# D groups first on TensorE, x_b tiles behind the gathers, and q weights made by VectorE for chunks 0 to 3

## The reference, cut to what matters

```
base = inputs                                   # (512, 40, 16): batch b, feature i, embedding d
curr = base
for Wk, bk in ((W0, b0), (W1, b1), (W2, b2)):
    z    = einsum('bid,bjd->bdij', base, curr)
    curr = einsum('bdij,ijh->bhd', z, Wk) + bk[None, :, None]
    logit.append(curr)
pooled = sum(concatenate(logit, axis=1), axis=-1)
out = pooled @ lin_w + lin_b                    # (512, 1)
```

## Time and profile before

| | us |
|---|---|
| median of 3 runs (185.47 to 185.96) | 185.86 |
| the profiled execution, its own time | 186.29 |
| its span from first to last instruction | 184.5 |
| TensorE busy (matmuls, 814) | 175.8 (95%) |
| VectorE busy | 151.8 (82%) |
| ScalarE busy | 73.9 (40%) |
| GpSimd busy | 16.2 (9%) |
| the 16 DMA engines, mean over the span | 204 GB/s |

### The profile page before, as it was taken

How to read it: one execution, slowest core, us unless ns; L and a number is a source line. 1 busy time by engine, 2 the same in 40 slices (tenths; PEclk the granted TensorE clock), 3 DMA queues, 4 the chain that set the end, 5 groups by cost and what they waited for, 6 DMA issues and landing times.

```text
span 184.5 us, 2573 instructions
## 1 busy us (share of the span) xinstructions
PE 175.8 (95%) x814; PEld 118.7 (64%) x814; DVE 151.8 (82%) x135; ACT 73.9 (40%) x79; POOL 16.2 (9%) x21
## 2 busy tenths in 40 slices
PE   7798998869999999999999999999999999999994
PEld 2364474546677777777777777777777777777760
DVE  0699698869999999999999999999999999300622
ACT  2554664124444624462446244534453445002001
POOL 3670010087000000000000000000000000000000
PEclk9999999999999999999999999999999999999999
DMA  6999997999797739774986597659765200000000
GB/s 192 379 409 411 412 219 218 231 406 397 230 324 233 234 122 321 247 227 124 331 230 228 126 322 235 223 135 329 228 219 128 99 0 0 0 0 4 0 0 0
DMA packets 11845, 37.71 MB, mean 204 GB/s; under 512 B 2305, under 2 KB 2941, under 8 KB 11838
## 3 DMA queue, kind: packets, MB, share of 16 engines
q1 hardware_dynamic: 11538, 37.38, 62.1%
q0 software_dynamic: 48, 0.16, 0.3%
q10 hardware_dynamic: 252, 0.09, 0.3%
HBM read 36.28 MB, written 1.33 MB: 204 GB/s over the span
## 4 chain that ended last, share of the span: by engine, by line
PE 79%; DMA 8%; SPq 3%; POOL 3%; issue 2%; DVE 1%; ACT 1%; DVEq 0%; ACTq 0%
PE q_ps L434 39%; PE c_ps L434 36%; DMA pair_sb<-d_dram 3%; DMA pair_sb<-w_pairs 3%; DMA d_dram<-w_d 2%; PE q_ps L518 2%; SPq L153 2%; POOL pair_sb L401 1%; POOL wq_low L424 1%; PE q_ps L443 1%; POOL wc_low L406 1%; DVE xb_z L246 1%; ACT z_high L324 1%; SPq L159 1%; PE c_ps L565 1%
## 5 line engine op out<-in xcount | busy, mean ns | idle before, releaser
L324 ACT ACTIVATE z_high<-xb_z 126x1024 fp32r<-126x1024 f32 x56 | 59.2, 1060 | 73.0 <-DVE xb_z L246 69.3
L253 DVE TENSOR_TENSOR z_low<-xb_z,z_high 126x1024 fp32r<-126x1024 f32 x56 | 68.9, 1232 | 1.1 <-ACT z_high L324 0.8
L246 DVE TENSOR_TENSOR xb_z<-x_a,xb_z 126x1024 f32<-126x1024 f32 x50 | 62.1, 1242 | 8.3 <-DMA xb_z<-xw 8.3
L434 PE MATMUL q_ps<-z_high,wq_high 126*101 126x512 f32 x108 | 34.1, 396 | 3.0 <-POOL wq_low L424 1.5
L434 PE MATMUL c_ps<-z_high,wc_high 126*101 126x512 f32 x112 | 35.5, 398 | 0.2 <-issue 0.2
L434 PE MATMUL c_ps<-z_high,wc_low 126*101 126x512 f32 x112 | 35.0, 394 | 0.0
L434 PE MATMUL c_ps<-z_low,wc_high 126*101 126x512 f32 x112 | 35.0, 394 | 0.0
L434 PE MATMUL q_ps<-z_high,wq_low 126*101 126x512 f32 x108 | 33.8, 394 | 0.0
L434 PE MATMUL q_ps<-z_low,wq_high 126*101 126x512 f32 x108 | 33.7, 393 | 0.0
L434 PEld LDWEIGHTS q_ps<-z_high,wq_high 126*101 126x101 f32 x108 | 17.7, 165 | 10.8 <-POOL wq_low L424 2.0
L434 PEld LDWEIGHTS c_ps<-z_high,wc_high 126*101 126x101 f32 x112 | 18.0, 165 | 9.0 <-issue 1.6
(11 more groups left out here) (56 smaller groups left out, 66.1 us busy)
## 6 DMA issues: line engine op xcount, KB each, us to landing
xb_z<-xw SPq DMA_DIRECT2D x50, 512.0 KB, 4.5
x_a<-xa SPq DMA_DIRECT2D x8, 512.0 KB, 5.0
w_d<-w2h SPq DMA_DIRECT2D x4, 512.0 KB, 7.4
w_post<-w1x SPq DMA_DIRECT2D x3, 512.0 KB, 10.0
d_dram<-w_d SPq DMA_DIRECT2D x4, 252.5 KB, 4.3
w_post<-w1x SPq DMA_DIRECT2D x1, 562.5 KB, 12.7
pair_sb<-d_dram SPq DMA_DIRECT2D x6, 82.9 KB
pair_sb<-w_pairs SPq DMA_DIRECT2D x1, 404.0 KB, 5.4
```

Source lines behind the costliest of these rows:

```text
L246: nc.vector.tensor_tensor(xb_z[0:K, c, :], x_a[0:K, u % 2, :], x_b, ALU.mult).then_inc(z_done, 1)
L253: nc.vector.tensor_tensor(z_low[0:K, m % SLOTS, :], xb_z[0:K, c, :], z_high[0:K, m % SLOTS, :].bitcast(fp32), ALU.subtract).then_inc(low_d ...
L324: nc.scalar.activation(z_high[0:K, m % SLOTS, :], xb_z[0:K, m % C, :], ACT.Copy).then_inc(high_done, 1)
L434: last = nc.tensor.matmul(ps[0:J, h * B:(h + 1) * B], w[0:K, c * J:(c + 1) * J], z[0:K, slot, h * B:(h + 1) * B], start=(c == 0 and k == 0 ...
```

## The change

It does three things. On TensorE all five D groups stand ahead of `c1_chunk(0, 1)`, with `select_xb(6)` between the second and the third. On the SP queue `load_xb(1, 2)` moves from behind the D stores to between the gathers of piece 0 and piece 1, and `load_xb(1, 3)` from there to behind piece 1. `first_weights` is now run twice on VectorE, for chunks 0, 1 at m = 10 and for chunks 2, 3 at m = 12, and now behind `split(m-1)`; GpSimd keeps chunks 4 to 6 and has semaphores of its own for them.

```diff
-PREP_AT = 9
+PREP_AT = (10, 12)
...
             store_d(sp, 0, LEFT + 4 * GI, 4 * GI, LOWER - 4 * GI, d_stored)
-            sp.wait_ge(low_done, 3)
-            load_xb(1, 2)
             sp.wait_ge(equals_cleared, 1)
...
             for side, t, piece in GATHER:
                 if piece == 1 and (side, t) == (0, 0):
-                    sp.wait_ge(low_done, 4)
-                    load_xb(1, 3)
+                    sp.wait_ge(low_done, 3)
+                    load_xb(1, 2)
                 if side == 0 or piece > 0:
                     gather_d(sp, side, t, piece)
-            for c in range(4, C):
+            for c in range(3, C):
                 sp.wait_ge(low_done, c + 1)
                 load_xb(1, c)
...
-            def first_weights():
+            def first_weights(i):
-                cols = slice(PREP_CUTS[0] * J, PREP_CUTS[1] * J)
-                dve.wait_ge(dpair_loaded[0], 16 * sum(g[2] == 0 for g in GATHER))
+                cols = slice(PREP_CUTS[i] * J, PREP_CUTS[i + 1] * J)
+                dve.wait_ge(dpair_loaded[i], 16 * sum(g[2] == i for g in GATHER))
...
-                    if m == PREP_AT:
-                        first_weights()
                     if m > 1:
                         split(it, m - 1)
+                    if m in PREP_AT:
+                        first_weights(PREP_AT.index(m))
...
-            for i in range(1, len(PREP_CUTS) - 1):
-                cols = slice(PREP_CUTS[i] * J, PREP_CUTS[i + 1] * J)
-                if PREP_CUTS[i] in WQ_CUTS:
-                    piece = WQ_CUTS.index(PREP_CUTS[i])
-                    pool.wait_ge(dpair_loaded[piece], 16 * sum(g[2] == piece for g in GATHER))
-                    pool.wait_ge(wq_ready, 1)
...
+            cols = slice(PREP_CUTS[2] * J, PREP_CUTS[3] * J)
+            pool.wait_ge(dpair_loaded[1], 16 * sum(g[2] == 1 for g in GATHER))
...
-                if m in PREP_CUTS[:-1]:
+                if m in PREP_CUTS[:2]:
                     pe.wait_ge(wq_ready, PREP_CUTS.index(m) + 1)
+                if m == PREP_CUTS[2]:
+                    pe.wait_ge(last_ready, 1)
...
             d_group(0)
             d_group(1)
-            c1_chunk(0, 1)
+            select_xb(6)
             d_group(2)
             d_group(3)
-            select_xb(6)
             d_group(4)
-            for m in range(2, LAG):
+            for m in range(1, LAG):
                 c1_chunk(0, m)
```

More of the change, by code:

```diff
@@ L133, in build @@
         wq_sums, wq_highs, wq_ready = sem("wq_sums"), sem("wq_highs"), sem("wq_ready")
+        last_sums, last_highs, last_ready = sem("last_sums"), sem("last_highs"), sem("last_ready")
         filled, equals_cleared = sem("filled"), sem("equals_cleared")
@@ L273, in split_x @@
                                         ALU.subtract).then_inc(xa_split, 1)
-            def first_weights():
-                cols = slice(PREP_CUTS[0] * J, PREP_CUTS[1] * J)
-                dve.wait_ge(dpair_loaded[0], 16 * sum(g[2] == 0 for g in GATHER))
+            def first_weights(i):
+                cols = slice(PREP_CUTS[i] * J, PREP_CUTS[i + 1] * J)
+                dve.wait_ge(dpair_loaded[i], 16 * sum(g[2] == i for g in GATHER))
                 nc.vector.tensor_tensor(q_sides[0:K, 0, cols], q_sides[0:K, 0, cols], q_sides[0:K, 1, cols],
                                         ALU.add).then_inc(wq_sums, 1)
-                dve.wait_ge(wq_sums, 1)
+                dve.wait_ge(wq_sums, i + 1)
                 nc.vector.tensor_copy(wq_high[0:K, cols], q_sides[0:K, 0, cols]).then_inc(wq_highs, 1)
-                dve.wait_ge(wq_highs, 1)
+                dve.wait_ge(wq_highs, i + 1)
                 nc.vector.tensor_tensor(wq_low[0:K, cols], q_sides[0:K, 0, cols], wq_high[0:K, cols].bitcast(fp32),
@@ L412, in _ @@
             store_d(pool, 1, 0, UPPER - LEFT, LEFT, d_stored_pool, (0, 32))
-            for i in range(1, len(PREP_CUTS) - 1):
-                cols = slice(PREP_CUTS[i] * J, PREP_CUTS[i + 1] * J)
-                if PREP_CUTS[i] in WQ_CUTS:
-                    piece = WQ_CUTS.index(PREP_CUTS[i])
-                    pool.wait_ge(dpair_loaded[piece], 16 * sum(g[2] == piece for g in GATHER))
-                    pool.wait_ge(wq_ready, 1)
[L419 to L425, removed]
+            cols = slice(PREP_CUTS[2] * J, PREP_CUTS[3] * J)
+            pool.wait_ge(dpair_loaded[1], 16 * sum(g[2] == 1 for g in GATHER))
+            nc.gpsimd.tensor_tensor(q_sides[0:K, 0, cols], q_sides[0:K, 0, cols], q_sides[0:K, 1, cols],
+                                    ALU.add).then_inc(last_sums, 1)
+            pool.wait_ge(last_sums, 1)
+            nc.gpsimd.tensor_copy(wq_high[0:K, cols], q_sides[0:K, 0, cols]).then_inc(last_highs, 1)
+            pool.wait_ge(last_highs, 1)
+            nc.gpsimd.tensor_tensor(wq_low[0:K, cols], q_sides[0:K, 0, cols], wq_high[0:K, cols].bitcast(fp32),
+                                    ALU.subtract).then_inc(last_ready, 1)
         @block.tensor
```

## The result

| | before | changed |
|---|---|---|
| median, us (4 runs each) | 185.73 | 194.68 |
| lowest to highest | 185.47 to 185.96 | 194.22 to 195.01 |
| profiled execution | 186.29 | 194.22 |
| its span | 184.5 | 192.4 |

The ratio is 1.048, with a 95% interval of 1.0449 to 1.0512: slower, as forecast, and 0.4 us from the forecast of 194.3. The two profiled executions are 7.9 us apart and the medians 8.95; the changed kernel's was the fastest of its four.

A forecast was written before the change was run, and what follows sets the result against it. The start of q_chunk(2) on TensorE was taken to set the end: 8.8 us later, less 0.3 of short gaps, net 8.5, gives a median of 194.3 us. The range takes in 191.8 and 196.9.

The forecast's parts named there:

- D groups first: TensorE's D groups ahead of c1_chunk(1): fourth copy 0.87 us earlier, gathers 0.9 us earlier, from 27.2 instead of 28.11.
- form(9): On VectorE: its x_b tile, in the slot of the old load_xb(1, 3), lands at 33.8 us; VectorE idles some 5 us.
- form(10): On VectorE: its tile, in the slot of the old load_xb(1, 4), lands at 37.7 us; start at 37.8.
- GpSimd beside VectorE: GpSimd's weights of chunks 4 to 6 stretch VectorE's work beside them: 0.5 us, bounds nothing and 1.3.
- The first weights: On VectorE behind form(10) and split(9): q_chunk(0) starts at 41.3 us, 41.8 with GpSimd's term, instead of 33.10.
- The clock: TensorE idles over 10 us before q_chunk(0) and falls to 1.2 GHz; return costs 1.7 us, bounds 0 and 3.4.
- The sum: TensorE's q_chunk(2) at 41.8 + 5.7 + 1.7 = 49.2 against 40.44, 8.8 us later; net 8.5 us.
- The rival in which the tiles don't gate: load_xb(1, 3) lands by 31 us, so q_chunk(0) starts at 34.5; 185.4 us, 2%.
- the one in which the clock stays up: Same wait, but TensorE restarts at full speed, q_chunk(2) at 47.6, 7.2 us later; 192.8 us, 10%.

The follow-up runs named there:

- the run that removes it: The changed kernel with 44 more warm-up matmuls on TensorE between c1_chunk(7) and q_chunk(0); ratio 1.0388, 192.86 us.

## Why the prediction was right, by its own steps

*D groups first* was the term that failed in its mechanism. The fourth copy came at 21.46, 0.3 us earlier than before and not 0.87, because D group 3 (the row at 20.34) waited for its piece of w1, which I had not looked at:

```profile
21.46 0.73 ACT L337 ACTIVATE w_d<-q_ps 128x505 f32<-128x505 f32 x2 [0.77 <-PE q_ps L518]
```

The third copy, ahead of that wait, did come 0.82 us earlier. Seven other traces with this TensorE order show the same wait; in the trace of the D groups alone there is none. The gathers came 0.5 us earlier, where I had taken 0.9. Even the 0.5 is not clear of what two executions differ by: with the D groups at their old place the first gather is at 27.42 in the run with the SP order alone and at 28.11 in the trace of before. (And the DMA engines' slackest microsecond beside the stores is the one from 27 to 28, at 75% and not 82%.)

*form(9)* was forecast at 33.8 and started at 33.23; *form(10)* at 37.8 and started at 37.65. The slots were right, and the old landing times a fair measure, but that it came out so closely is in part luck. The gathers came 0.4 us later than I had taken, and the tiles made up for it by landing 4.3 and 5.3 us after their issue, where the old ones took 5.3 and 6.1. In the four other traces with this SP order form(9) starts between 32.85 and 34.18 and form(10) between 37.01 and 38.41.

*GpSimd beside VectorE* was put at 0.5 us and was 0.74, 0.11 on form(10) and 0.62 on split(9). VectorE ran beside GpSimd's subtraction and not its add, which stood alone:

```profile
36.59 0.81 POOL L414 TENSOR_TENSOR pair_sb<-pair_sb 126x303 f32<-126x303 f32 x1 [13.29 <-DMA pair_sb<-d_dram]
...
37.98 1.68 POOL L419 TENSOR_TENSOR wq_low<-pair_sb,wq_high 126x303 fp32r<-126x303 f32 x1
```

The size of 0.5 was luck, because I read rows 9 wrongly. The Trainium skill, SBUF — State Buffer, section Who interferes with whom, would have the loser blocked for a whole instruction. I took that to mean the full 1.8 us of GpSimd's add and so set it aside. But the recorded 1.8 us can hold GpSimd's own wait. The same subtraction takes 0.84 us where it begins just ahead of VectorE's form (the row at 38.37 above) and 1.68 here, where it begins 0.92 us before form(10) gives way to split(9). It ends at 39.66, 0.76 us behind the start of split(9), which takes 0.62 longer. In the rows of before the add ends at 40.35 + 1.82 = 42.17, 0.78 us behind the start of the form at 41.39, which takes 0.65 longer. So the rows agree with that section: VectorE loses what is left of GpSimd's instruction once its own turn comes, in these rows at most some 0.8 us, and not 1.8.

*The first weights* follow: q_chunk(0) forecast at 41.8, measured 41.87.

*The clock* was put at 1.7 us and cost 1.26 by the run that removes it: a size that was too large, and the mechanism held. TensorE worked at the lower level from 41.87 to about 44.7; I had taken the time of the warm-up, 3.4. The Trainium skill, TensorE: Matmul & The Clock Gate, section Why this matters for your kernels, warned that an idle gap between bursts of matmuls throws the clock back; this trace agrees, with 0.50 in the idle stretch from 34.5 to 41.8.

*The sum* put q_chunk(2) at 49.2, measured 48.78: 0.1 us too little up to q_chunk(0) and 0.5 too much behind it. The gaps behind it gave back 8.34 - 7.93 = 0.4 us, forecast 0.3. For the profiled execution that makes 194.8 forecast and 194.22 measured. The medians lie closer, 194.3 and 194.68, because the execution of before was 0.6 us above its kernel's median and that of the changed kernel 0.5 below its own; that is luck. (The median of 185.86 with 8.5 is 194.4 and not 194.3.) The rival in which the tiles don't gate fell at form(10), the one in which the clock stays up fell at the 0.50.

## What to carry to other kernels

Before work is moved behind another step on an in-order engine, look at what that step waits for: the moved work inherits the wait, even if its own input landed long ago. A load moved behind other transfers arrives about when the load that had that slot arrived; here the trace of before told that to within 2 us, and the executions differed by 1.4 among themselves. TensorE's waits of 3.27 to 10.38 us in these runs cost, beside themselves, 1.3 to 1.7 us each in the matmuls behind them, and 2.8 us in the trace of the changed kernel with the old SP order, an execution that was itself 2.3 us over its median. Work that fills one engine's idle time is free only if no neighbour that starts on the same event holds it up: VectorE's cast took 0.79 us instead of 0.27 beside GpSimd.

## What the runs showed of the hardware that I had not expected

The clock can fall after the work has resumed, so that the price of a wait stands behind it. In the run with the SP order alone TensorE was idle for 3.84 us, q_chunk(0) started at full clock, and only then did it fall:

```profile
31.40:35.20 3.80, 0.00 (x1) 0.01 (x1) 2.28 (x5) 1.06 (x1) 0.00 (x0) 1.00 1.08 212
35.20:35.80 0.60, 0.60 (x3) 0.47 (x4) 0.60 (x1) 0.00 (x0) 0.00 (x0) 1.00 0.97 348
35.90:39.20 3.30, 3.30 (x9) 2.18 (x9) 2.49 (x3) 0.93 (x1) 3.15 (x4) 0.50 1.03 410
39.30:42.00 2.70, 2.70 (x13) 1.91 (x13) 2.70 (x3) 0.42 (x2) 2.56 (x3) 1.00 1.03 411
```

Nine matmuls are recorded in the 3.3 us at the lower level against 13 in the following 2.7, and by the starts of the pairs the wait of 3.84 us cost 1.63 us more behind it. It was no single case: in the run with the first weights back behind form(9), TensorE waited 4.53 and 3.27 us, started both times at full clock (1.00 from 32.0 to 36.3 and from 43.7 to 46.9), and both times the clock stood at 0.50 soon after, from 37.0 to 40.2 and from 47.3 to 50.5.
